# Image stage of a vision block: head scores from doubled row tiles in two round-mode products, and a new order of work

## The reference, cut to what matters

```python
h = _L0_tok_ref(x, scharr)                      # gray, two 3x3 filters, abs, sum: 32 x 256 x 256
h = concatenate([cls_tok, h], axis=1)           # 257 rows per image, 256 wide
h = h + attn(layernorm(h))                      # x_proj = silu(x @ W1 + b1); u, v, q, k = split(x_proj, 4)
...
scores = einsum("bqhd,bkhd->bhqk", qh, kh)      # 16 heads of 16
attn = silu(scores) / S
av = einsum("bhqk,bkhd->bqhd", attn, vh)
y = layernorm(av * u, gamma, beta) @ W2 + b2
...
ri = concatenate([xf, stats(xf)], -1)           # mean, std, min, max, l2, share near zero
h = gelu(ri @ r1_w.T + r1_b); probs = softmax(h @ r2_w.T)    # router: two experts a row, capacity 321
```

## Time and profile before

| | |
|---|---|
| median of the runs | 1599.02 us |
| the profiled execution's own time | 1595.68 us |
| its span, first to last instruction | 1593.7 us |
| mean granted TensorE clock, share of full | 0.924 |
| TensorE matmuls busy | 1368.8 us, 86% |
| VectorE busy | 1069.6 us, 67% |
| ScalarE busy | 894.2 us, 56% |
| DMA moved | 177.27 MB |

### The profile page before, as it was taken

How to read it: one execution, slowest core, us unless ns; L and a number is a source line. 1 busy time by engine, 2 the same in 40 slices (tenths; PEclk the granted TensorE clock), 3 DMA queues, 4 the chain that set the end, 5 groups by cost and what they waited for, 6 DMA issues and landing times. The chain is left out here.

```text
span 1593.7 us, 32947 instructions
## 1 busy us (share of the span) xinstructions
PE 1368.8 (86%) x12125; PEld 1067.1 (67%) x12125; DVE 1069.6 (67%) x2947; ACT 894.2 (56%) x1595; POOL 420.2 (26%) x370
## 2 busy tenths in 40 slices
PE   3899999999999999999984623338999999999996
PEld 2566666666666666666653613238999999999996
DVE  4366666666666666666644487877777777777773
ACT  1567667677776767767662125234555555555552
POOL 0112212112121221211200000012455555555553
PEclk8899999999999999999997555578999999999999
DMA  7333424334244343443203230004555656556552
GB/s 220 99 99 96 131 75 124 109 90 131 79 120 113 85 131 82 117 115 83 63 28 124 96 3 0 1 17 161 153 175 155 191 143 191 156 175 179 154 160 26
DMA packets 128702, 177.27 MB, mean 111 GB/s; under 512 B 19966, under 2 KB 116996, under 8 KB 124484
## 3 DMA queue, kind: packets, MB, share of 16 engines
q1 hardware_dynamic: 111172, 154.38, 32.0%
q0 software_dynamic: 17408, 21.25, 8.1%
HBM read 134.17 MB, written 41.41 MB: 110 GB/s over the span
## 5 line engine op out<-in xcount | busy, mean ns | idle before, releaser
L671 ACT ACTIVATE at<-ps_s 128x1024 f32<-128x1024 f32 x256 | 248.7, 1028 | 42.3 <-PE ps_s L550 42.3
L197 PE MATMUL ps_s<-xet,whi 128*128 128x322 f32 x640 | 206.7, 323 | 17.9 <-issue 10.9
L1802 POOL DMA_INDIRECT out_rows<-ye,slot_token x96 | 151.3, 1576 | 226.2 <-ACT ye L1660 216.6
L198 PE MATMUL ps_s<-xet,wlo 128*128 128x322 f32 x640 | 201.0, 314 | 0.0
L199 PE MATMUL ps_s<-xet,whi 128*128 128x322 f32 x640 | 199.6, 312 | 0.0
L1629 ACT ACTIVATE sg<-ps_s 128x322 f32<-128x322 f32 x160 | 70.5, 440 | 170.3 <-PE ps_s L199 170.2
L1724 DVE TENSOR_TENSOR wlo<-raw,whi 128x640 fp32r<-128x640 f32 x192 | 156.9, 818 | 1.3 <-ACT whi L1639 1.3
L550 PE MATMUL ps_s<-q,k 32*128 32x256 f32 x2048 | 146.6, 400 | 4.5 <-ACT at L671 1.4
L197 PEld LDWEIGHTS ps_s<-xet,whi 128*128 128x128 f32 x640 | 122.3, 191 | 26.0 <-issue 26.0
L197 PE MATMUL ps_av<-whi,hs 128*128 128x256 f32 (+1 forms) x480 | 134.5, 280 | 2.9 <-DVE wlo L1724 2.9
L566 PE MATMUL ps_av<-at,uv 128*16 128x257 f32 x2048 | 136.0, 383 | 0.3 <-ACT at L729 0.3
(11 more groups left out here) (356 smaller groups left out, 3405.9 us busy)
## 6 DMA issues: line engine op xcount, KB each, us to landing
raw<-in_wexp SPq DMA_DIRECT2D x32, 1280.0 KB, 6.2
halo<-gray_dram SPq DMA_DIRECT2D x96, 288.0 KB
xb<-in_x SPq DMA_DIRECT2D x64, 384.0 KB, 4.7
raw<-in_wexp SPq DMA_DIRECT2D x32, 640.0 KB, 6.0
gray_dram<-g SPq DMA_DIRECT2D x32, 256.0 KB, 3.3
out_rows<-h SPq DMA_DIRECT2D x64, 128.0 KB, 6.6
token_rows<-xf SPq DMA_DIRECT2D x64, 128.0 KB, 3.9
pre_dram<-pre SPq DMA_DIRECT2D x32, 128.0 KB, 4.9
```

The source lines that it names most:

```text
L197: nc.tensor.matmul(o, lh, rh, start=first, stop=False)
L198: nc.tensor.matmul(o, ll, rh, start=False, stop=False)
L671: nc.scalar.activation(at[:, t, 2 * i:2 * i + 2, :, 0:R].rearrange("p j k q -> p (j k) q"), ps_s[i][:, :, :, :].rearrange("p j k q -> p (j ...
L1802: nc.gpsimd.indirect_dma_start(out=out, out_offset=bass.IndirectOffsetOnAxis(ap=slot_token[0:w, 3 * m + st:3 * m + st + 1], axis=0), in_=y ...
```

## The change

- **Scores.** q and k are kept once, in `qn` and `kn`. VectorE's `stream_shuffle` doubles each head's 16 rows within its row tile (`dup`: even heads, then odd). For k, `stack_k` rounds `dup` to f32r and turns the second 16 rows of each row tile into the low part, so that a row tile holds one head's high part over its low part. For q, ScalarE's `hi_q` makes the high part in all 32 rows and VectorE's `split_q` the low part. `score` then does two f32r products for each of the 8 places (q high, q low) and sums them in PSUM: 16 instructions where float32 had 16.
- **Class scores** read `qn` and `kn`: 4 float32 products in the place of 6.
- **Router.** The mean's weights are folded into `r1ws` in the set-up; the statistics are held three times (`stw`, high, low and high part), so that the last product is one of f32r; standard deviation and norm come from the variance of h2 on GpSimd, and the statistics pass over xf is gone from VectorE.
- **Order.** TensorE, ScalarE, VectorE and GpSimd have a new order in the step; the rows' statistics and turning of xf move from image d to image e. `conv` of the first half now begins the step, and `router_pre` stands second to last in it. SyncE's body is unchanged.
- **Expert stage.** The up weights of experts 0 and 1 are split before the first product; the rows' turning is signalled in two halves; `split_down` of the second piece stands before the last gate; the last expert's down products start on four of the five pieces.
- A few small instructions in set-up and class stage follow from the above.

```diff
-        UNITS = ["B0", "A0", "E", "D0", "D1", "G0", "B1", "D2", "A1", "D3", "B2", "B3", "B4", "D4"]
-        LAG = {"E": 0, "G": -2, "D": -1, "B": 1, "A": 2}
+        UNITS = ["A0", "B0", "D0", "D1", "E", "F0", "B1", "D2", "B2", "A1", "B3", "D3", "G0", "B4"]
+        LAG = {"E": 0, "G": -2, "F": -2, "D": -1, "B": 1, "A": 2}
...
             def cls_scores(n, r, m):
 
                 bank_free(pe, n, "E")
+                pe.wait_ge(qk_act, 2 * m + 2)
                 for a in range(2):
-                    nc.tensor.matmul(bank("E")[32 * a:32 * a + 32, 0:R], cw[:, a, :], q2[r % 2][:, a, :], start=True, stop=True)
-                for e in range(2):
-                    for a in range(2):
-                        last = nc.tensor.matmul(bank("E")[64 + 32 * a:96 + 32 * a, 0:R], cw[:, 2 + a, :], k2[r % 2][:, e, a, :],
-                                                start=e == 0, stop=e == 1)
+                    nc.tensor.matmul(bank("E")[32 * a:32 * a + 32, 0:R], cw[:, a, :], qn[:, a, :], start=True, stop=True)
+                for a in range(2):
...
             def score(n, r, m, t):
                 if t == 0:
-                    pe.wait_ge(qk_act, 2 * m + 2)
+                    pe.wait_ge(q_ready, m + 1)
+                    pe.wait_ge(k_ready, m + 1)
                 wait(pe, attn, 8 * m + 2 * t)
                 e, a = t // 2, t % 2
                 for kt in range(2):
-                    for j in range(4):
-                        last = nc.tensor.matmul(ps_s[j // 2][:, j % 2, kt, :], k2[r % 2][32 * j:32 * j + 32, e, a, kt * 128:kt * 128 + 128],
-                                                q2[r % 2][32 * j:32 * j + 32, a, :], start=True, stop=True)
+                    for hl in range(2):
+                        for j in range(4):
+                            row = slice(32 * j, 32 * j + 32)
+                            last = nc.tensor.matmul(ps_s[j // 2][:, j % 2, kt, :], kd[r % 2][row, e, a, kt * 128:kt * 128 + 128],
+                                                    qd[r % 2][row, hl, e, a, :], start=hl == 0, stop=hl == 1)
...
                 a, b, c, d, e = n + 2, n + 1, n, n - 1, n - 2
+                if has(a):
+                    conv(n, r, a, 0, "A0")
                 if has(b):
                     transposes(n, "B0", xn, xn_done, b + 1, xt_ps)
                 if has(c):
                     score(n, r, c, 0)
-                if has(a):
-                    conv(n, r, a, 0, "A0")
+                if has(d):
+                    back(n, r, d, 0)
+                    back(n, r, d, 1)
                 if has(c):
                     cls_scores(n, r, c)
                     score(n, r, c, 1)
-                    pe.wait_ge(cls_act, c + 1)
-                    wait(pe, av_out, 4 * c)
-                if has(d):
-                    back(n, r, d, 0)
+                if has(e):
+                    transposes(n, "F0", xf, xf_done, e + 1, xft_ps)
                 if has(c):
                     cls_turn(c)
-                if has(d):
-                    back(n, r, d, 1)
-                if has(e):
-                    stats_turn(n, e)
                 if has(b):
                     proj_qk(n, b, 0, "B1")
-                if has(e):
-                    router_pre(n, e)
                 if has(c):
                     weighted(n, r, c, 0)
                 if has(d):
                     transposes(n, "D2", z, z_done, d + 1, zt_ps)
+                if has(b):
+                    proj_qk(n, b, 1, "B2")
                 if has(c):
+                    weighted(n, r, c, 1)
                     score(n, r, c, 2)
                 if has(a):
                     conv(n, r, a, 1, "A1")
+                if has(b):
+                    proj_uv(n, b, 0, "B3")
                 if has(d):
                     proj_out(n, d)
-                if has(c):
-                    weighted(n, r, c, 1)
-                if has(b):
-                    proj_qk(n, b, 1, "B2")
+                if has(e):
+                    stats_turn(n, e)
                 if has(c):
                     score(n, r, c, 3)
-                if has(b):
-                    proj_uv(n, b, 0, "B3")
-                if has(c):
                     weighted(n, r, c, 2)
                 if has(b):
                     proj_uv(n, b, 1, "B4")
-                if has(d):
-                    transposes(n, "D4", xf, xf_done, d + 1, xft_ps)
+                if has(e):
+                    router_pre(n, e)
                 if has(c):
                     weighted(n, r, c, 3)
 
@@ -679,18 +693,56 @@
 
                 def silu_q():
                     act.wait_ge(qk_ps, 2 * b + 1)
+                    wait(act, q_dup, b)
+                    wait(act, cls_ps, b)
...
+                def hi_q():
+                    act.wait_ge(q_dup, b + 1)
+                    wait(act, scores, 4 * (b - 1))
+                    nc.scalar.activation(qd[(r + 1) % 2][:, 0, :, :, :].rearrange("p e t q -> p (e t q)"),
+                                         dup[:, :, :, :].rearrange("p e t q -> p (e t q)"), ACT.Copy).then_inc(q_hi, 1)
...
+                def stats_hi():
+                    act.wait_ge(st_ps, e + 1)
+                    wait(act, r1_ps, e)
+                    nc.scalar.activation(stt[:, :], bank("G0")[0:96, 256:512], ACT.Copy).then_inc(st_hi, 1)
+
+                def keep_pre():
+                    act.wait_ge(r1_ps, e + 1)
+                    wait(act, pre_out, 16 * e)
+                    nc.scalar.activation(pre[:, :], bank("G0")[:, 0:256], ACT.Copy).then_inc(pre_done, 1)
...
-                    av_copy(0)
+                    silu_scores(1)
                 if has(d):
                     turned_hi(zt, "D2", zt_ps, w2_ps, d, d, zt_hi)
-                if has(c):
-                    silu_scores(2)
+                if has(b):
+                    hi_q()
+                    silu_k()
                 if has(a):
                     abs_edges(1)
                 if has(c):
-                    av_copy(1)
-                if has(b):
-                    silu_k()
-                if has(c):
-                    silu_scores(3)
+                    silu_scores(2)
+                    av_copy(0)
+                if has(e):
+                    stats_hi()
                 if has(b):
                     silu_uv(0)
                 if has(c):
+                    av_copy(1)
+                    silu_scores(3)
+                if has(e):
+                    keep_pre()
+                if has(c):
                     av_copy(2)
-                if has(d):
-                    act.wait_ge(xf_done, d + 1)
-                    wait(act, st_done, d)
-                    nc.scalar.activation(axf[:, :, :], xf[:, :, :], ACT.Abs).then_inc(axf_done, 1)
-                    turned_hi(xft, "D4", xft_ps, r1_ps, d, d, xft_hi)
+                    av_copy(3)
...
+                def shuffled(src, ready, done):
+                    dve.wait_ge(qk_act, ready)
+                    nc.vector.memset(spare[:, :], 0.0)
+                    for par in range(2):
+                        half = [16 * par + i for i in range(16)]
+                        last = nc.vector.stream_shuffle(dup[:, par, :, :].rearrange("p t q -> p (t q)"),
+                                                        src[:, :, :].rearrange("p t q -> p (t q)"), half + half)
+                    last.then_inc(done, 1)
+
+                def double_q():
+                    wait(dve, k_ready, b)
+                    shuffled(qn, 2 * b + 1, q_dup)
+
+                def split_q():
+                    dve.wait_ge(q_hi, b + 1)
+                    nc.vector.tensor_tensor(qd[(r + 1) % 2][:, 1, :, :, :].rearrange("p e t q -> p (e t q)"),
+                                            dup[:, :, :, :].rearrange("p e t q -> p (e t q)"),
+                                            qd[(r + 1) % 2][:, 0, :, :, :].rearrange("p e t q -> p (e t q)").bitcast(f32),
+                                            ALU.subtract).then_inc(q_ready, 1)
+
+                def double_k():
+                    dve.wait_ge(q_ready, b + 1)
+                    shuffled(kn, 2 * b + 2, k_dup)
+
+                def stack_k():
+                    flat_k = kd[(r + 1) % 2][:, :, :, :].rearrange("p e t q -> p (e t q)")
+                    flat_d = dup[:, :, :, :].rearrange("p e t q -> p (e t q)")
+                    dve.wait_ge(k_dup, b + 1)
+                    nc.vector.tensor_copy(flat_k, flat_d).then_inc(k_hi, 1)
+                    dve.wait_ge(k_hi, b + 1)
+                    nc.vector.scalar_tensor_tensor(flat_k, flat_k.bitcast(f32), cst[:, CUP:CUP + 1], flat_d,
+                                                   ALU.mult, ALU.add).then_inc(k_ready, 1)
...
+                    gray_green(dve, gm)
+                if has(e):
+                    turned_lo(xft, bank("F0")[:, :], xft_hi, e, xft_done)
+                if has(d):
+                    norm_z()
+                if grayed(gm):
+                    gray_blue(dve, gm)
```

(30 more changed lines are left out.)

## The result

The changed kernel takes **1838.79 us** (median of 4 runs, 1831.24 to 1841.09). The kernel before took 1599.13 us (4 runs, 1597.01 to 1600.01) beside it. The ratio is 1.149, with an interval of 1.146 to 1.153. The forecast was 1770 us, in a range of 1700 to 1885.

The account below looks back on a forecast made before the run. TensorE's order was taken as the bound before, and a chain through the halo's load after the change. 1599 + 184 (27 steps, each 6.8 us longer) - 13 (the rest) = 1770 us, range 1700 to 1885 us.

Parts of the forecast that it names:

- that chain: Image stage: convolution, step up to router, copy of pre, its store, halo's load, next convolution; 29.3 us per step against 24.8.
- The step: Image stage: 29.3 us from convolution to convolution plus 2.3 us lost to low clock, 31.6 us, 6.8 more than now.
- TensorE's work: Image stage: falls from 24.8 to 22.1 us per step through scores (1.65), class scores (0.4), router (0.33), a wait (0.3).
- The halo's load: SyncE's load for the next convolution: 7.0 us from issue to landing, low end 5 us, 9 us at the most.
- The clock: TensorE behind each 7.2 us stall: 5 us at half clock, 2.3 us lost; shortest 1.6, longest 6.5 us lost.
- rival 1: Image stage: clock stays low through the q product, 35.8 us a step, 1883 us in total; chance 0.2.
- The count: Image stage: the late halo holds up steps n = 2 to 28, 27 steps, +184 us.
- The rest: Part-filled steps -6 us, expert stage waits cut to 2.5, 2.5 and 2 us, class stage and set-up under 1; together -13 us.
- their uncertain prices cost nothing here: Image stage: VectorE's 21.3 and ScalarE's 18.1 us per step have 8 us to spare, so their prices cost nothing.
- 2: Clock does not fall or returns at once, or halo lands in 5 us with short dip: 29.3 us a step, 1708 us; chance 0.15.
- 3: Image stage: halo is in time and the kernel gets faster, steps of 22.5 to 23.5 us, 1537 us; chance 0.06.
- Rival 4: Scores: f32r row tiles no faster than float32 ones, 1.65 us more per step, 1815 us; chance 0.04.

Follow-up runs that it names:

- Experiment 1: Changed kernel with SyncE's halo load ahead of its wait for pre and the store of pre: 1503.62 us; same swap in the kernel before: 1599.32 us.
- experiment 7: Four more VectorE reductions of 512 elements per image: 1567.64 us in the changed kernel with halo load first, 1875.41 us in the changed kernel itself.
- the fill: Changed kernel with 56 unused f32r products behind the last weighted sum of 27 steps: 1720.73 us; with 24 products 1860.83 us, with 40 1826.55 us.
- experiment 6: Changed kernel with halo load first, scores as one float32 product per place, q's low part left out: 1552.15 us.

## Why the prediction was right, and what was sized wrong

**Sign and mechanism** held: the router product late in TensorE's step, the store of pre ahead of the halo's load on SyncE, the convolution first in the next step. Of the signs that were named, the stall (7.9 us, forecast 6 to 8), its releaser and the low clock came as said. The starts of successive first convolutions lie 34.4 us apart, outside the 31 to 33 that were named. Experiment 1 removes that chain alone and gets 335 us back; 256 us was the loss over 27 steps, and 2.9 x 27 = 79 us the gain under it.

**The step** was forecast at 31.6 us and measured at 34.4. By its three terms:

| term of the sum | forecast | measured | from |
|---|---|---|---|
| TensorE's work at full clock | 22.1 | 21.8 | experiment 1 |
| idle before the convolution | 7.2 | 7.9 | windows after |
| lost to the clock | 2.3 | 4.7 | 26.5 - 21.8 |

**TensorE's work** was right to 0.3 us, and with it the prices of the scores (0.41 us of a set by the forecast; 0.41 in the timelines), of the class scores and of the router.

**The halo's load** was the smaller error. I took 7.0 us from issue to landing, from the last traffic in the earlier trace rows. That row does show the data's end, and the run without other stores puts it at 6.6 us as well. But the consumer starts only 1.3 us after the last byte. The Trainium skill (DMA: Bandwidth & Descriptors, Anatomy of one DMA — SWDGE (gpsimd) path) puts most of a transfer's fixed cost behind the last byte, in the receipt of the write. It says so of transfers that GpSimd issues; this one is SyncE's, and its nearly empty windows from 746.7 to 748.0 agree. I had also taken the upper bound of 9 us for a load that shares the engines with h2 and xf; the sharing turned out to cost nothing.

**The clock** was the larger one. I took 5 us at half and 2.3 us lost. The windows show 9.9 us at half behind one stall, and 4.7 us were lost per step on average. I weighed three rows against each other and took the middle, mostly because of the row from 938.8 to 942.2. I misread that row: it is not filled by transposes alone, since the last 0.6 us of its work are two products of class scores:

```profile
941.52 0.59 PE L1298 MATMUL ps_s<-cst,clsk 32*128 32x8 f32 x2
```

What I did not ask is whether one length holds for every step. It does not. Three of the 26 steps had the short return that I took as the least, and 14 had 8 to 11 us. In the other nine the clock was still at half when the q product began, as rival 1 has it for all steps, and in three of them through all of it. So the measured mean of 4.7 us lies between the forecast's 2.3 and rival 1's 6.5. The rows before could not tell which of their lengths would come how often.

**The count.** I had 27 steps of 6.8 us, 184. It came to 26 steps of 9.6 us and one of 5.4 (its convolution at 103.86, the next at 134.07, 30.2 us, with the clock still up): 256 us.

**The rest** was -13 and came to -10 us (the profiled spans, 1839.3 and 1593.7 us, are 245.6 apart, less 256). The expert stage gave 9.2 us: from its first turning to the span's end it took 521.5 us before (from 1072.20) and 512.3 after (from 1327.03), against 7 forecast. That leaves about 1 us for the part-filled steps, from which I had expected 6. TensorE in the expert stage, after:

```profile
1327.03 1.34 PE L1759 MATMUL ps_f<-cst,xe 128*128 128x128 f32 x6 [9.72 <-DMA xe<-token_rows,slot_token]
1329.51 0.61 PE L201 MATMUL ps_s<-xet,whi 128*128 128x322 f32 x1 [1.15 <-DVE xet L1906]
...
1822.39 0.36 PE L201 MATMUL ps_av<-whi,hs 128*128 128x256 f32 x1 [0.46 <-DVE wlo L1889]
```

The waits of 3.76 and 2.88 us in the earlier trace rows are 1.15 and 0.46 now, and the one of 3.21 us is gone.

**VectorE and ScalarE** were forecast at 21.3 and 18.1 us a step and take 20.8 and 17.6. Groups of the trace after, 400 to 600 us: a shuffle takes 0.75 us, where the reduction of the earlier trace rows had made me say 0.68; the split 1.23 and the rounding of k 0.68:

```profile
L876 DVE STREAM_SHUFFLE dup<-qn 128x512 f32<-128x512 f32 x12 | 8.5, 755 | 0.0
...
L886 DVE TENSOR_TENSOR qd<-dup,qd 128x1024 fp32r<-128x1024 f32 x6 | 7.4, 1226 | 0.7
...
L899 DVE CAST kd<-dup 128x1024 fp32r<-128x1024 f32 x6 | 4.1, 679 | 0.0
```

That "their uncertain prices cost nothing here" was too strong: 2.7 us more on VectorE cost 0.9 us in a step of the chain, in experiment 7, since an engine with 13 us to spare in a step can still be late at one place of it.

**Rivals.** 1 (1883 us) is 44 us above the result, and the forecast is 69 us below it: by the total, rival 1 was the nearer; 2 (1708 us) is nearly what the fill made of the kernel, and would have come true had the clock not fallen; 3 is experiment 1 but for its price: I gave a step without the chain 22.5 to 23.5 us for VectorE's waits, and it took 21.9. Rival 4 is excluded by experiment 6.

## What to carry to other kernels

When work is moved on the compute engines, read the DMA-issuing queue as one more engine whose order did not move: a wait in it that used to be over in time holds back every transfer behind it, and a load for the next step behind a store of this step's last result closes a chain. The repair cost nothing here and turned 15% slower into 6% faster. In a sum, take a load's price up to its consumer's start and not to its last byte, and price a stall with the clock in its wake, as a range: stalls of about 8 us with the same work behind them were followed here by 3.5 to 15 us at half. And a change of order that is tried on two engines out of three measures the third one's order.

## What the runs showed of the hardware

- The loss to the clock did not grow with the idle time: 4.2, 5.1 and 4.7 us per step for 2.9, 4.9 and 7.9 us idle, none for 1.0 (means over 26 steps). Idle time that is filled halfway bought nothing (1860.8 us with 24 products, against 1838.8 without).
- 56 useless products per step made a kernel 118 us faster: they ran in idle time, and the clock stayed up behind them.
- Behind stalls of about 8 us, in one kernel and with the same order of work behind them, the clock was at half for 3.5 to 4.0 us in three steps, 8 to 11 in 14 and 12 to 15 in nine.
- In the kernel before with its halo late, stalls of 1.8 to 3.6 us were followed by 3.4 us at half in 11 of 28 cases and by full clock in 17, and the length of the stall did not sort them.
- A load of 864 KB in rows of 1 KB took 7.7 us from its issue to its consumer with 512 KB of stores beside it and 7.9 us without them, in the steps shown. In the latter, 1.3 us of it came after its last data.
